# An attention and expert block on one core: expert slots moved into attention's last slot, the first lots cut anew, and the mask, state and read-out put in another order

## The chip, the cores and the metric

The kernel runs on one core of a Trainium2 chip, in one launch. The time is device microseconds of one execution, and the figure compared is the median of several. Five engines work side by side, each with its own queue in program order: PE (TensorE, matrix products), DVE (VectorE), ACT (ScalarE), POOL (GpSimd) and SP (SyncE, which here only issues DMAs). They wait for one another by semaphores.

## The reference

Four steps, each with a residual, on x of 4 x 1024 tokens by 128 (4096 tokens):

```
x = x + attn_a(layernorm(x))   # linear attention, H = 64: phi = elu + 1,
                               # S += k v^T, z += k, o = S q / max(z . q, 1e-6), then W_o
x = x + ffn(layernorm(x))      # 8 experts, top 1: gate * (relu(x W1[e] + b1[e]) W2[e] + b2[e])
x = x + attn_b(layernorm(x))   # 8 x 512: decayed running sum over tokens, mixed; sigmoid(r) * (v Wo)
x = x + ffn(layernorm(x))      # the same experts again
```

The expert of a token is the largest of its 8 router logits, which depend on the token's own row after attention; D_FF is 512. The reference computes all experts for all tokens and masks, the kernel only the chosen one.

## The kernel before

The 4096 tokens are 32 tiles of 128 rows (NT), in 8 groups of 4 tiles (NG, GT). **Attention** runs in slots k = 0 to 8 (`attn_slot(k)` on each engine, written out by hand). Slot k projects group k, forms scores and state of group k - 1, and reads out group k - 2 (`project_out`). On PE the order is: query and key projection (`project_qk`, L1661), read-out (L1763, L1767), scores and turns (L1693, L1681, L1704), transposes, value projection (L1670), state update and product within the chunk (L1714, L1723), product with the carried state (`read_inter`, L1743), and the count of chosen experts (`count`, L1644). On DVE it is: `add_attention` (dmax L979, then the new rows L996), the mask (L1118), then the choice of experts for batch k - 3 mixed with the statistics of group k - 2 and the addition of the state (L1131), then phi (qk, L1139), the placing of batch k - 3 (`placed`, L955 to L966), and the scan of z (L1146). ACT evacuates PSUM, takes exp and relu for phi, normalizes the next group (`norm`) and copies the read-out (`evac_o`, L702). POOL computes zq (L513) and the row scales (L505), and sends tiles of rows to their place in the sorted array in memory by indirect DMA (L532). SENDS_OF_ATTENTION says which tiles in which slot: 0 to 12 by slot 7, then 13, 14 to 19 in slot 8, 20 to 27 after it; the last four go among the expert slots.

**Experts** run in 39 slots (ST) of 128 sorted rows. A slot is: SP loads the rows (xs), DVE normalizes them (xsn, L1381), PE turns them (L1887), ACT copies the turned rows (xsT, L796), PE forms the first product (L1897), ACT, from slot 9 on with DVE, applies relu (hT, L801), PE forms the second product (L1911), DVE adds it to the row (L1411) and POOL scatters the result (L555). ACT also copies each slot's weights ahead (w1s, L719). Slots belong to lots (STAGES): a lot may be loaded when all rows of its batches are sent and its table (`table_step`: which expert and which tile each slot has) is done. In the first layer the lots have 9, 12 and 18 slots and end with batches 3, 6 and 7, so the first lot needs tiles 0 to 15. The first table is made by DVE in slot 8 (L1276 to L1316). PE does dummy products (`keep_clock`, L1780) in slot 8 and ahead of the first expert turn. After the first layer the rows come back from memory, the mixing runs in slots of its own, and a second set of 39 expert slots follows, with lots of 5, 8, 8 and 18.

## Time and profile before

| | |
|---|---|
| median of 3 runs | 287.8 us (287.49 to 288.69) |
| the profiled execution | 288.31 us, its span 286.6 us |
| PE busy | 270.5 us, 94% of the span |
| DVE busy | 227.2 us, 79% |
| POOL busy | 219.0 us, 76% |
| ACT busy | 183.8 us, 64% |
| mean granted clock of PE | 0.988 |
| attention slots | from 12.65 to about 70 us |
| first layer's experts | to about 151 us |
| mixing, then the second layer's experts | to the end |

The span is that of the trace; 1.7 us of the execution lie around it. Starts are counted from the span's start. The shares are means over stages in which different engines wait.

### The profile page before, as it was taken

The numbers are of one execution on the slowest core, as the hardware profiler recorded it, in microseconds if no ns is written. First come the engines' busy times: TensorE is split into PE (matmuls) and PEld (weight loads), VectorE is DVE, ScalarE is ACT, GpSimd is POOL, SyncE is SP. The second block draws the span as 40 slices with busy tenths as digits, with TensorE's granted clock in tenths as the row PEclk, the third lists the DMA queues.
The fourth block names the chain that finished last, engine by engine and source line by source line (L and its number), as shares of the span: only waits on it lengthen the run. The fifth ranks groups of instructions, "written<-read, shape, count | busy, mean of one in ns | idle before, by whom it ended". The sixth has DMA issues, their size and how long they took to land.

```text
span 286.6 us, 8102 instructions
## 1 busy us (share of the span) xinstructions
PE 270.5 (94%) x2343; PEld 239.6 (84%) x2343; DVE 227.2 (79%) x1030; ACT 183.8 (64%) x564; POOL 219.0 (76%) x304
## 2 busy tenths in 40 slices
PE   7989999987899999999999799999899999999994
PEld 7766666654598999999994488898699999999994
DVE  4797999997786987788771589999947988777873
ACT  2686666531599788888870276563289976676661
POOL 3956288777868898886553888888778888888875
PEclk9999999998999999999999999999899999999999
DMA  5799950011413655331103800101324244332210
GB/s 133 212 260 321 172 88 31 28 41 53 120 39 86 131 109 114 100 80 47 39 18 75 225 1 0 49 29 40 90 64 115 76 119 101 108 94 71 66 42 4
DMA packets 32652, 25.73 MB, mean 90 GB/s; under 512 B 6129, under 2 KB 28914, under 8 KB 32609
## 3 DMA queue, kind: packets, MB, share of 16 engines
q1 hardware_dynamic: 27456, 16.54, 25.5%
q0 software_dynamic: 4576, 8.57, 9.0%
q8 instruction: 20, 0.33, 0.5%
q14 instruction: 24, 0.19, 0.2%
q10 hardware_dynamic: 576, 0.10, 0.2%
HBM read 14.60 MB, written 11.57 MB: 91 GB/s over the span
## 4 chain that ended last, share of the span: by engine, by line
PE 63%; DVE 18%; DMA 5%; SPq 4%; issue 3%; POOL 3%; ACT 2%; DVEq 0%; ACTq 0%; POOLq 0%
PE pair L1911 21%; PE pair L1897 15%; PE bank L1897 7%; PE bank L1887 3%; SPq L374 3%; PE pair L1831 2%; DVE rows L996 2%; PE bank L1780 2%; DVE stats L1011 2%; PE pair L1763 2%; PE pair L1824 2%; PE pair L1661 2%; DMA rows<-x_mid 2%; DVE am L1118 1%; DVE sc L1220 1%
## 5 line engine op out<-in xcount | busy, mean ns | idle before, releaser
L1911 PE MATMUL pair<-w2s,hT 128*128 x624 | 82.7, 276 | 0.1
L532 POOL DMA_INDIRECT sorted<-rows,place x64 | 66.5, 1039 | 18.2 <-issue 14.9
L1911 PEld LDWEIGHTS pair<-w2s,hT 128*128 128x128 f32 x624 | 75.7, 192 | 0.4 <-issue 0.2
L1897 PE MATMUL pair<-xsT,w1s 128*128 128x128 f32 x406 | 57.7, 278 | 0.9 <-ACT xsT L796 0.9
L1897 PEld LDWEIGHTS pair<-xsT,w1s 128*128 128x128 f32 x406 | 51.5, 194 | 1.9 <-DVE tm L1229 1.0
L719 ACT COPY w1s<-w1all 128x516 f32 x78 | 49.7, 638 | 0.6 <-issue 0.4
L555 POOL DMA_INDIRECT x_mid<-ys,xs x39 | 38.5, 986 | 13.9 <-DVE ys L1421 9.4
L555 POOL DMA_INDIRECT out<-ys,xs x39 | 38.6, 989 | 9.1 <-issue 7.2
L796 ACT COPY xsT<-bank 128x128 f32<-128x128 f32 x78 | 20.8, 267 | 37.2 <-PE bank L1887 36.3
L1411 DVE SCALAR_TENSOR_TENSOR ys<-pair,xs 128x128 f32<-128x128 f32 x78 | 27.0, 347 | 21.3 <-PE pair L1911 20.9
L801 ACT ACTIVATE hT<-pair,w1s 128x128 f32<-128x128 f32 x117 | 34.8, 375 | 1.1 <-PE pair L1897 1.1
L801 ACT ACTIVATE hT<-bank,w1s 128x128 f32<-128x128 f32 x109 | 32.6, 377 | 0.0
L1897 PE MATMUL bank<-xsT,w1s 128*128 128x128 f32 x218 | 31.1, 278 | 0.4 <-ACT xsT L796 0.4
L1392 DVE SCALAR_TENSOR_TENSOR xs<-b2b,xs 128x128 f32<-128x128 f32 x78 | 27.3, 351 | 4.8 <-issue 2.7
L1381 DVE TENSOR_SCALAR xsn<-xs 128x128 f32<-128x128 f32 x78 | 28.0, 363 | 2.9 <-DMA xs<-sorted 2.9
L1897 PEld LDWEIGHTS bank<-xsT,w1s 128*128 128x128 f32 x218 | 28.0, 196 | 0.6 <-ACT xsT L796 0.6
L1401 DVE TENSOR_SCALAR hT<-pair,w1s 128x128 f32<-128x128 f32 x86 | 27.6, 346 | 0.7
L505 POOL TENSOR_TENSOR rows<-veps,neg_half 128x4 f32<-128x4 f32 x16 | 17.2, 1072 | 8.8 <-ACT veps L675 7.7
L563 POOL MEMSET idle_row<- 1x320 f32 x60 | 21.9, 364 | 0.0
L1887 PE MATMUL bank<-ident,xsn 128*128 128x128 f32 x78 | 21.5, 275 | 0.3 <-DVE xsn L1381 0.3
L1831 PE MATMUL pair<-wp,sc 128*128 128x256 f32 x64 | 16.3, 379 | 0.0
L1824 PE MATMUL pair<-wx,xnT 128*128 128x256 f32 x64 | 15.7, 388 | 0.6 <-DVE xnT L1201 0.6
(184 smaller groups left out, 499.3 us busy)
## 6 DMA issues: line engine op xcount, KB each, us to landing
xs<-sorted SPq DMA_DIRECT2D x78, 66.0 KB, 2.3
rows<-x_mid SPq DMA_DIRECT2D x8, 260.0 KB, 5.1
w1all<-in_L_ffn_W_b SPq DMA_DIRECT2D x8, 258.0 KB, 6.0
rows<-in_L_attn_a_x SPq DMA_DIRECT2D x16, 128.0 KB, 2.7
w2s<-in_L_ffn_W SPq DMA_DIRECT2D x8, 256.0 KB, 5.3
sorted<-pad SPq DMA_DIRECT2D x30, 66.0 KB
sorted<-rows,place POOLq DMA_INDIRECT x64, 2.6
x_mid<-ys,xs POOLq DMA_INDIRECT x39, 2.6
```

The source lines that it names most:

```text
L532: pool.indirect_dma_start(sorted_rows[l], bass.IndirectOffsetOnAxis(ap=place[:, t:t + 1], axis=0), rows[:, t, :], None).then_inc(s_sent[l] ...
L555: pool.indirect_dma_start(x_new[l], bass.IndirectOffsetOnAxis(ap=xs[b][:, IDC:IDC + 1].bitcast(I32), axis=0), ys[b][:, 0:(XM, D)[l]], None ...
L719: nc.scalar.copy(w1s[i % NW][:], w1all[:, bass.ds(e, 1), :].rearrange("p o f -> p (o f)")).then_inc(s_w1, 1)
L801: last = nc.scalar.activation(hT[i % NB][:, c], bank[2 + i % 2][:, c * P:(c + 1) * P], ACT.Relu, bias=w1s[i % NW][:, DF + c:DF + c + 1])
L1381: nc.vector.tensor_scalar(xsn[i % NB][:], xs[b][:, 0:D], xs[b][:, MEAN:MEAN + 1], xs[b][:, RSTD:RSTD + 1], ALU.subtract, ALU.mult).then_in ...
L1392: nc.vector.scalar_tensor_tensor(out=xs[b][:, 0:D], in0=b2b[:, bass.ds(e, 1), :].rearrange("p o d -> p (o d)"), scalar=xs[b][:, GATE:GATE ...
L1401: last = nc.vector.tensor_scalar(hT[i % NB][:, c], bank[4 + i % 2][:, f:f + P], w1s[i % NW][:, DF + c:DF + c + 1], 0.0, ALU.add, ALU.max)
L1411: nc.vector.scalar_tensor_tensor(out=ys[b][:, 0:D], in0=bank[6 + i % 2][:, 0:P], scalar=xs[b][:, GATE:GATE + 1], in1=xs[b][:, 0:D], op0=AL ...
L1831: last = nc.tensor.matmul(mix_to(g, j), sc[g % 2][:, j * P:(j + 1) * P], wp[:].rearrange("p w d -> p (w d)"), start=False, stop=(j % 2 == ...
L1887: nc.tensor.transpose(bank[0][:, 0:P], xsn[i % NB][:], ident[:]).then_inc(s_xsT, 1)
L1897: mm = nc.tensor.matmul(bank[2 + 2 * half + i % 2][:, c * P:(c + 1) * P], w1s[i % NW][:, f:f + P], xsT[i % NB][:], start=True, stop=True)
L1911: mm = nc.tensor.matmul(bank[6 + i % 2][:, 0:P], hT[i % NB][:, c], w2s[:, bass.ds(e, 1), c, :].rearrange("p o d -> p (o d)"), start=(c == ...
```

## The change

First layer only, with the line numbers of each program in the fences:

- **Lots.** The first layer gets the second's lots: 5, 8, 8 and 18 slots, that end with batches 2, 4, 6 and 7. The first needs tiles 0 to 11 only. SENDS_OF_ATTENTION is as before. Four tables are made in place of three.
- **Tables.** The first table's steps are dealt into slots 6 and 7 of attention (five and four steps), the second's into slot 8.
- **Slot 8.** DVE normalizes the rows of expert slots 0 and 1 right behind the mask. PE turns the first of them ahead of `read_inter`, and does the first product and the second turn ahead of the last `project_out`. ACT does the copies of both and the first relu in slot 8, ahead of the exp of batch 5 and `row_veps` of batch 6. The dummy products go (five in all).
- **All attention slots.** `project_qk(k + 1)` stands at the end of slot k, ahead of the count. The counts go to bank 2 and wait for `evac_v`; the value projection waits for the placing that read them, and `project_out` no longer does. On DVE the state is added ahead of the maximum of the logits, the mask is one instruction in place of two, and z's scan stands ahead of `placed`. On ACT `evac_o` stands ahead of `norm`.
- **Placing.** `placed` of batch 5 moves behind the last `add_attention`; its count behind the last `project_out`.
- **Start.** SP issues the six loads of the mixing weights behind x of group 3, ahead of x of groups 4 to 7. On DVE the moments of group 4 move into slot 0, those of group 6 into slot 1.

```diff
-STAGES = [[(3, 9), (6, 12), (7, 18)], [(2, 5), (4, 8), (6, 8), (7, 18)]]
+STAGES = [[(2, 5), (4, 8), (6, 8), (7, 18)], [(2, 5), (4, 8), (6, 8), (7, 18)]]
-        attn_counts = bank[7][:, 2 * YC:2 * YC + (GT + 1) * E]
+        attn_counts = bank[2][:, HW + P:HW + P + (GT + 1) * E]
...
                 for g in range(2, NG):
                     load_x(l, g)
+                    if l == 0 and g == 3:
+                        for dst, src in ((rwo, rw_o), (rwr, rw_r), (rwv, rw_v)):
+                            sp.dma_start(dst[:], src).then_inc(s_wmix, 16)
+                        for i, v in enumerate((time_decay, mix_v, mix_r)):
+                            sp.dma_start(vec[:, i:i + 1], v.rearrange("(h o) -> h o", o=1)).then_inc(s_wmix, 16)
...
+                if k == NG:
+                    copy_w1(0, 0)
                 if 0 <= k - 1 < NG:
                     evac_kv(k - 1)
+                if k == NG:
+                    evac_rows(0, 0)
+                    copy_w1(0, 1)
+                    evac_o(LASTG)
+                    relu(0, 0)
+                    evac_rows(0, 1)
+                    lexp(0, AS, LASTG - 2)
+                    row_veps(AS, LASTG - 1)
+                    return
...
                 row_stats(AS, g, 1)
                 bias_logits(0, AS, b)
                 row_stats(AS, g, 2)
+                add_state(g + 1)
                 max_logit(0, b)
...
-                if g + 1 < LASTG:
-                    add_state(g + 1)
...
                 if k == NG:
-                    table_sums(0, 0)
-                    table_experts(0, 0)
-                    add_state(k - 1)
-                    table_places(0, 0)
+                    normed_rows(0, 0)
+                    normed_rows(0, 1)
+                    measure_choose_and_list()
+                    return
...
                 phi(k)
+                scan_z(k)
                 if k - 3 >= 0:
                     placed(0, AS, k - 3)
-                scan_z(k)
                 if k == 0:
+                    first_moments(4)
+                    mix_weights(0)
                     first_moments(5)
+                if k == 1:
                     first_moments(6)
-                    mix_weights(0)
-                if k == 1:
                     first_moments(7)
...
                 if 0 <= k - 1:
                     updates_and_intra(k - 1)
+                if k == NG:
+                    turn_rows(0, 0)
                 if 0 <= k - 1:
                     read_inter(k - 1)
+                if k == NG:
+                    after(pe, AS["posb"], 2 * (LASTG - 3) + 1)
+                    first_product(0, 0)
+                    turn_rows(0, 1)
+                    return
+                if k + 1 < NG:
+                    project_qk(k + 1)
                 if 3 <= k < NG:
-                    pe.wait_ge(AS["xnew"], k - 1)
+                    pe.wait_ge(AS["v"], k + 1)
                     count(AS, k - 3, attn_counts)
-                if k == NG:
-                    count(AS, k - 3, bank[1])
...
                 if l == 0:
                     project_out(LASTG)
-                    keep_clock(3)
+                    count(AS, LASTG - 2, bank[1])
+                    pe.wait_ge(s_w2, 16 * (1 + E))
```

`measure_choose_and_list` is the choice of batch 5 and the statistics of group 6, with the end of the first table, the state, and all nine steps of the second table among them, in the order of the second layer's `choose_measure_and_list`.

On PE, in attention's last slot and behind it, before: vT is turned, then dummies on w2s, the state's update, the masked scores with kt, the state's product, the count; and after the read-out of the last group (wox) come more dummies, and only then the experts' turn (xsn) and first product (w1s).

```order
L1704 MATMUL bank<-ident,vT 128x128 x3
L1780 MATMUL bank<-w2s,ident 128x512 x2
L1714 MATMUL pair<-kt,vt 64x64 x2
L1723 MATMUL pair<-am,kt 64x128 x4
L1743 MATMUL pair<-qk,state 64x128 x4
L1644 MATMUL pair<-oh,before 128x32
```

```order
L1763 MATMUL pair<-wox,ob 128x137 x2
L1767 MATMUL pair<-ones_col,zq 128x1 x2
L1763 MATMUL pair<-wox,ob 128x137 x2
L1767 MATMUL pair<-ones_col,zq 128x1 x2
L1780 MATMUL bank<-w2s,ident 128x512 x3
L1887 MATMUL bank<-ident,xsn 128x128
L1897 MATMUL pair<-xsT,w1s 128x128 x4
L1887 MATMUL bank<-ident,xsn 128x128
L1897 MATMUL bank<-xsT,w1s 128x128 x4
L1887 MATMUL bank<-ident,xsn 128x128
```

And in the changed program:

```order
L1762 MATMUL bank<-ident,vT 128x128 x3
L1772 MATMUL pair<-kt,vt 64x64 x2
L1781 MATMUL pair<-am,kt 64x128 x4
L1943 MATMUL bank<-ident,xsn 128x128
L1801 MATMUL pair<-qk,state 64x128 x4
L1953 MATMUL pair<-xsT,w1s 128x128 x4
L1943 MATMUL bank<-ident,xsn 128x128
L1819 MATMUL pair<-wox,ob 128x137 x2
L1823 MATMUL pair<-ones_col,zq 128x1 x2
L1819 MATMUL pair<-wox,ob 128x137 x2
L1823 MATMUL pair<-ones_col,zq 128x1 x2
L1700 MATMUL pair<-oh,before 128x32
```

The first expert turn stands ahead of the state's product, the first product and second turn ahead of the last read-out, and the dummies are gone.

On ACT, in the same slot, before: the last kt and vt, the exp of batch 5 (le), the read-out (ob), veps of batch 6, then the first weights (w1s) and the first turned rows (xsT).

```order
L695 COPY kt<-pair 128x256
L696 COPY vt<-bank 128x384
L668 ACTIVATE le<-ld 128x32
L702 COPY ob<-pair 128x256
L675 ACTIVATE veps<-rows 128x4
L348 TENSOR_LOAD etab
L719 ISA
L719 COPY w1s<-w1all 128x516
L796 COPY xsT<-bank 128x128
L348 TENSOR_LOAD etab
```

And in the changed program:

```order
L696 COPY kt<-pair 128x256
L697 COPY vt<-bank 128x384
L803 COPY xsT<-bank 128x128
L348 TENSOR_LOAD etab
L720 ISA
L720 COPY w1s<-w1all 128x516
L703 COPY ob<-pair 128x256
L808 ACTIVATE hT<-pair,w1s 128x128 x4
L803 COPY xsT<-bank 128x128
L669 ACTIVATE le<-ld 128x32
L676 ACTIVATE veps<-rows 128x4
```

veps of batch 6, which POOL's row scale waits for, now stands behind the first relu (hT) and the second turned rows.

On DVE, around the start of slot 0 (phi gives qk, zT is the scan), before, with moments as stats and mv:

```order
L859 BN_STATS stats<-rows 128x6 x4
L864 BN_AGGR mv<-stats 128x2 x4
L1261 TENSOR_SCALAR whole<-capt 1x8 x2
L1139 SCALAR_TENSOR_TENSOR qk<-ex,rl 128x512
L1146 SCALAR_TENSOR_TENSOR zT<-ones_col,qk 128x256
L859 BN_STATS stats<-rows 128x6 x4
L864 BN_AGGR mv<-stats 128x2 x4
L859 BN_STATS stats<-rows 128x6 x4
L864 BN_AGGR mv<-stats 128x2 x4
L1361 COPY rwoT<-pair 128x128
L1362 TENSOR_SCALAR mix_c<-vec 128x2
```

And in the changed program:

```order
L1313 TENSOR_SCALAR whole<-capt 1x8 x2
L1194 SCALAR_TENSOR_TENSOR qk<-ex,rl 128x512
L1201 SCALAR_TENSOR_TENSOR zT<-ones_col,qk 128x256
L865 BN_STATS stats<-rows 128x6 x4
L870 BN_AGGR mv<-stats 128x2 x4
L1413 COPY rwoT<-pair 128x128
L1414 TENSOR_SCALAR mix_c<-vec 128x2
L865 BN_STATS stats<-rows 128x6 x4
L870 BN_AGGR mv<-stats 128x2 x4
L1173 TENSOR_TENSOR am<-pair,causal 128x512
L1422 TENSOR_SCALAR wx<-pair,vec 128x128
```

One set of moments has moved from ahead of qk to behind the scan, and the mask (am) is one instruction.

## Rows read from the trace of the kernel before

**Rows 1.** The page, part 1: busy us, share of the span, instructions.

```profile
PE 270.5 (94%) x2343; PEld 239.6 (84%) x2343; DVE 227.2 (79%) x1030; ACT 183.8 (64%) x564; POOL 219.0 (76%) x304
```

**Rows 2.** Timeline, attention slot 6: start us, duration us, engine, line, operation.

```profile
49.09 0.16 DVE L979 TENSOR_SCALAR dmax<-pair 128x4 f32<-128x4 f32 x1 [0.43 <-PE pair L1767]
...
52.95 0.65 PE L1743 MATMUL pair<-qk,state 64*64 64x128 f32 x8 [0.35 <-DVE state L1131]
...
55.94 0.16 DVE L979 TENSOR_SCALAR dmax<-pair 128x4 f32<-128x4 f32 x1 [0.47 <-PE pair L1767]
```

**Rows 3.** Timeline, attention's last slot and the first expert slots, PE and DVE.

```profile
61.24 0.50 PE L1763 MATMUL pair<-wox,ob 64*128 64x137 f32 x4 [0.56 <-DVE posb L955]
...
62.35 0.16 DVE L979 TENSOR_SCALAR dmax<-pair 128x4 f32<-128x4 f32 x1
...
63.90 0.74 DVE L1118 TENSOR_TENSOR am<-pair,causal 128x256 f32<-128x256 f32 x2
...
70.36 0.16 DVE L979 TENSOR_SCALAR dmax<-pair 128x4 f32<-128x4 f32 x1 [0.86 <-PE pair L1767]
...
71.92 0.59 DVE L1381 TENSOR_SCALAR xsn<-xs 128x128 f32<-128x128 f32 x2
...
72.53 0.35 DVE L1392 SCALAR_TENSOR_TENSOR xs<-b2b,xs 128x128 f32<-128x128 f32 x1
...
74.69 0.19 DVE L931 TENSOR_TENSOR oh<-rev,top 128x32 bf16<-128x32 f32 x1
...
74.80 1.13 PE L1897 MATMUL pair<-xsT,w1s 128*128 128x128 f32 x8 [0.45 <-ACT xsT L796]
...
77.63 1.14 PE L1911 MATMUL pair<-w2s,hT 128*128 x8
```

**Rows 4.** Timeline, the first attention slots, DVE and PE.

```profile
10.49 0.87 DVE L859 BATCH_NORM_STATS2 stats<-rows 128x6 f32<-128x128 f32 x4
...
12.65 0.69 DVE L1139 SCALAR_TENSOR_TENSOR qk<-ex,rl 128x512 f32<-128x512 f32 x1 [0.41 <-ACT rl L682]
...
16.02 0.33 PE L1875 MATMUL pair<-ident,rwo 128*128 128x128 f32 x1 [0.89 <-DMA vec<-in_L_attn_b_time_mix_r]
...
19.38 0.99 DVE L1139 SCALAR_TENSOR_TENSOR qk<-ex,rl 128x512 f32<-128x512 f32 x1
...
22.24 0.13 DVE L979 TENSOR_SCALAR dmax<-pair 128x4 f32<-128x4 f32 x1
```

**Rows 5.** Timeline, DVE in the second layer's slot with a table.

```profile
200.06 0.16 DVE L1321 TENSOR_SCALAR cover<-cumt 1x8 f32<-1x8 f32 x1
...
201.17 0.16 DVE L909 TENSOR_REDUCE mx<-lg 128x4 f32<-128x32 f32 x1
```

**Rows 6.** Timeline, ACT and POOL in the passage to the experts.

```profile
68.52 0.21 ACT L675 ACTIVATE veps<-rows 128x4 f32<-128x4 f32 x1 [0.27 <-DVE rows L1017]
...
72.66 1.06 POOL L532 DMA_INDIRECT sorted<-rows,place  x1 [0.30 <-issue]
...
76.24 1.15 ACT L801 ACTIVATE hT<-pair,w1s 128x128 f32<-128x128 f32 x4
...
77.25 0.65 ACT L719 COPY w1s<-w1all 128x516 f32 x1
```

**Rows 7.** Timeline, the opening of the second lot: PE, POOL, DVE.

```profile
79.50 0.27 PE L1887 MATMUL bank<-ident,xsn 128*128 128x128 f32 x1
...
85.38 0.96 POOL L532 DMA_INDIRECT sorted<-rows,place  x1 [0.30 <-issue]
...
90.93 0.35 DVE L1381 TENSOR_SCALAR xsn<-xs 128x128 f32<-128x128 f32 x1 [2.29 <-DMA xs<-sorted]
...
91.33 0.33 PE L1887 MATMUL bank<-ident,xsn 128*128 128x128 f32 x1 [0.30 <-DVE xsn L1381]
```

**Rows 8.** Windows: busy us of each engine, granted clock, DMA share, GB/s.

```profile
66.00:69.00 3.00, 1.09 (x17) 0.79 (x19) 2.65 (x19) 0.70 (x3) 1.67 (x3) 1.00 0.14 47
69.00:73.00 4.00, 4.00 (x20) 2.54 (x19) 3.05 (x15) 0.62 (x1) 3.19 (x4) 0.57 0.37 95
```

More of the change, by code:

```diff
@@ L1095, in measure_choose_and_add_state @@
                 scale_logits(0, AS, b)
+                if b == LASTG - 4:
+                    table_step(0, 0, "tiles")
+                if b == LASTG - 3:
+                    table_step(0, 0, "experts")
+                    table_step(0, 0, "jumps")
                 row_stats(AS, g, 1)
@@ L1109, in measure_choose_and_add_state, with measure_choose_and_list @@
                 row_moments(AS, g, 2)
+                if b == LASTG - 4:
+                    table_step(0, 0, "past")
+                    table_step(0, 0, "jump")
                 one_hot(0, AS, b)
                 row_moments(AS, g, 3)
+            def measure_choose_and_list():
+                b, g = LASTG - 2, LASTG - 1
+                sum_logits(b)
+                dve.wait_ge(AS["xnew"], g + 1)
+                table_step(0, 0, "cover")
+                row_stats(AS, g, 0)
+                scale_logits(0, AS, b)
+                table_step(0, 0, "taken")
+                row_stats(AS, g, 1)
+                table_step(0, 1, "tiles")
+                bias_logits(0, AS, b)
+                table_step(0, 1, "round")
+                row_stats(AS, g, 2)
+                add_state(g + 1)
+                max_logit(0, b)
+                table_step(0, 0, "behind")
+                row_stats(AS, g, 3)
+                table_step(0, 1, "sum")
+                lead_logits(0, AS, b)
+                dve.wait_ge(AS["st2"], 2 * g + 1)
+                row_moments(AS, g, 0)
+                table_step(0, 1, "past")
+                table_step(0, 1, "jump")
+                rank_leaders(0, AS, b)
+                row_moments(AS, g, 1)
+                table_step(0, 1, "experts")
+                top_rank(0, b)
+                table_step(0, 1, "jumps")
+                row_moments(AS, g, 2)
+                one_hot(0, AS, b)
+                table_step(0, 1, "skips")
+                row_moments(AS, g, 3)
+                table_step(0, 1, "places")
             def mask_scores(g):
@@ L1572, in _ @@
             norm_half()
-            for g in range(2, 5):
+            for g in range(2, 4):
                 first_moments(g)
```

177 lines of the change are left out of this document (85 added, 92 removed).

## The prediction, made before the changed kernel ran

> **What bounds the kernel now.** I read the busy shares of the page first: TensorE (PE) is busy 94% of the span, VectorE (DVE) 79%, GpSimd (POOL) 76%, ScalarE (ACT) 64% [rows 1]. This is an average over stages, so I read the timeline by stage. In the attention part one slot, counted from dmax to dmax, takes 6.85 us (slot 6: 49.09 to 55.94), and two engines wait little in it: PE stands 0.35 us before the read of the state (L1743), waiting for DVE's state, and DVE stands 0.47 us before dmax (L979), waiting for PE's read-out [rows 2]. So PE's own work is about 6.85 - 0.35 = 6.5 us a slot and DVE's about 6.85 - 0.47 = 6.4 us: whoever gets a wait removed hands the bound to the other 0.1 us later. Then comes the passage to the experts: from dmax of attention's last slot (62.35) to the first second product (77.63) it is 15.28 us [rows 3]. From there PE runs without a gap at 1.9 us a slot, but for one stall at the opening of the second lot (turn at 91.33) [rows 7]. So the layer is a chain of DVE and PE to 62.35, a passage of waits, and then PE alone; what changes the end is when the second products begin, how fast PE's clock is there, and whether each lot's rows are in time. The second layer isn't edited, and I let it move as a block.
>
> **Part 1, the start of attention.** The six mix loads go ahead of x of group 4, so PE no longer waits for them (0.89 us before L1875 [rows 4]). This gives little: ACT is the next in line, since the router weights now stand behind the projection of slot 1, and I find the transposes of slot 1 at the same time within 0.2 us. The cost is on DVE. The moments of group 4 lie now in a hole: they start at 10.49 and DVE waits again for 0.41 us at 12.65 for ACT's rl [rows 4]. They move behind that point, where DVE goes without long waits up to dmax of slot 2 at 22.24. One set of moments is 0.87 of stats and 0.38 of aggregates, 1.25 us [rows 4]. Against it: qk of slot 1 takes 0.99 us while POOL's zq runs beside it, and 0.69 us at 12.65 [rows 4]; zq(0) now comes later, because the moments of group 5, for which POOL's scales of groups 4 and 5 wait ahead of it, now stand behind those of group 4 and the mix weights; so this 0.3 us is saved. Sum **+1.0 us** at dmax of slot 2; bounds 0 (if a wait that I don't see absorbs it) and +1.4.
>
> **Part 2, slots 3 to 5.** DVE adds the state before the maximum and the last stats, 0.4 us earlier, so PE's 0.35 us go; the mask in one instruction of 512 columns in place of two saves DVE one fixed part, 0.06 us. The slot becomes PE's 6.5 us. **-0.36 us** each in three slots, -1.1 together; I take -1.15 since one of the three had a wait of this kind and one for the one-hot. Bounds 0 and -1.4 (DVE's floor). The read-out copied ahead of the norm delays ACT's exp and relu by up to the norm; they end just before PE's turn of k needs them, so I cost it at nothing, at worst 0.2 a slot.
>
> **Part 3, slots 6 and 7.** Here the first table is dealt in. In the second layer a stretch with four such steps, nine instructions from cover to the maximum, takes 1.11 us [rows 5], 0.12 each in the mean; the steps are its smallest, so I take 0.08 to 0.1 each. Five steps in slot 6 make DVE's slot 6.4 - 0.06 + 0.4 = 6.7 (before 6.85), four in slot 7 make it about 6.75 where before it was 62.35 - 55.94 = 6.41 [rows 2, 3]: -0.1 and **+0.33**. DVE is the bound here, so all of it counts. The scan of z also stands before the placing now, so that POOL's zq runs beside DVE's pick. The row of slot 1 says that such a neighbour can cost 0.3 us (0.99 against 0.69 [rows 4]); I add **+0.3** for both slots, bounds 0 and 0.8.
>
> The Trainium skill, "SBUF — State Buffer", section "Who interferes with whom", says that a DVE instruction with two SBUF inputs and a GpSimd instruction that reads SBUF block one another for their length. By that rule alone pick would wait for most of zq in each slot and the sum would be 0.5 us worse; the trace agrees for qk, and shows no pick beside a zq.
>
> Parts 1 to 3: +1.0 - 1.15 - 0.1 + 0.33 + 0.3 = **+0.4 us**: dmax of slot 8 at 62.75.
>
> **Part 4, the passage.** Counted from dmax of slot 8. The mask ends at 64.64 - 62.35 - 0.06 = 2.23 [rows 3]. Two normed rows, 0.35 each less overlap: 2.85; I see no wait for their load, since lot one needs only tiles 0 to 11 (sent by slot 7) and a table that is done in slot 7. Sum of logits, then cover to the maximum in 1.11 [rows 5]: 4.05; state 0.2: 4.25. PE reads it in 0.65 (52.95 [rows 2]): 4.95; first product 1.1 (1.13 [rows 3]): 6.05; turn 0.1; read-out 1.11 (61.24 to 62.35 [rows 3]): 7.25. The read-out (project_out(7)) now stands behind expert work, and DVE, through with its list at about 6.3, waits 0.9 us for it. From dmax to the new rows' end 71.92 - 70.36 = 1.56, with the pipeline's tail 1.65: 8.9. Placing of batch 5, five small instructions, 0.65: 9.55. From hidden(0) to the one-hot of batch 6 74.88 - 72.53 = 2.35, less a pause of 0.1 [rows 3]: 11.8; with 0.2 us for the register load ahead of hidden: 12.0. Count and semaphores 0.2: the first second product at **12.2** in place of 15.28, **-3.1 us**. What went are the table and the placing ahead of DVE's last add_attention, and the first turn and product behind it, with the dummies; what is late next is the one-hot of batch 6, as the count ahead of the second product waits for it. Bounds -3.5 (DVE's dependent chain faster) and -2.0 (a semaphore of 0.1 us for each of ten hops more).
>
> ACT: row_veps(6) stands behind relu(0,0), which waits for the first product. It is at 6.05 + 1.15 (four relus [rows 6]) + 0.5 = 7.7 in place of 68.52 - 62.35 = 6.17. POOL's scale waits for it, and tiles 17 to 19 are queued behind: tile 19 is sent at 11.6 in place of 72.66 - 62.35 = 10.31 [rows 6]. Afterwards ACT stands for row_veps(7) until DVE's moments of group 7 (about 14.0), and in these slots ACT is as long as PE (1.15 of relu, 0.65 of copy [rows 6] and the evacuation): a slip of **+0.2 us**.
>
> **Part 5, the lots.** From sending a lot's last tile to the turn of its first slot it is 91.33 - 85.38 = 5.95 us [rows 7]. Second lot: 11.6 + 5.95 = 17.55, wanted by PE at 12.2 + 5.6 = 17.8, so just in time. Third lot: tile 27 goes as now at about 85.4 on POOL, which loses 1.3 us by the veps and no longer has to wait as long for the placing of batch 6; wanted four slots later than now, so it fits by 5 us. The stall of the second lot goes: turns stand at 79.50 and 91.33, six slots, 11.83 us, of which 6 x 1.9 = 11.4 are slots: **-0.45 us**. Last lot as now with 2 us less of slack; POOL's scatters catch up before the layer's end.
>
> **Part 6, PE's clock.** The granted clock was 1.00 from 66 to 69 us with PE busy 1.09 of 3 us, and 0.57 in the mean over 69 to 73: it stood at its lower level, 1.2 GHz, for about 3.4 us, then came back to 2.4 [rows 8]. Today that falls on the dummy products. Now they are gone, and PE has 1.7 us idle ahead of turn(2) and again 1.5 ahead of the count, between 8.6 and 12.0. I expect the same fall, and the lower level to last into the first two slots. A low stretch of 3.4 us costs 1.7 if all of it is work; about a quarter lies on the idle part: **+1.3 us**. Bounds 0 and 3.4 (two stretches). The Trainium skill, "TensorE: Matmul & The Clock Gate", section "HAM oscillation", says that PE left idle between bursts drops to half its clock and begins the next burst cold. The trace agrees with it [rows 8]. By that rule alone both idle pieces count, the term is its bound of 3.4, and the sum ends 2.1 us higher, at 288.1.
>
> **Sum**, against the profiled execution (288.31 us, span 286.6): +0.4 - 3.1 + 0.2 - 0.45 + 1.3 = -1.65, so 286.65. That execution lies 0.5 us above the median of the three runs, 287.8; against the median I get 286.1, and say **286.0**.
>
> **Rivals.** (a) The clock holds or is low only while PE idles: 1.3 less, 284.7. For it: the work in the passage is denser than between 66 and 68.5 us. Against it: two idle pieces one after the other. Chance 0.2. (b) The clock stays low for a second stretch, since the first finds PE half idle: 1.7 more, 287.7. Chance 0.15. (c) The gain of the attention slots doesn't come, or the mid-passage hops are dearer: parts 2 and 4 at their near bounds, +1.5, 287.5. Chance 0.1. (d) The change doesn't do what it says: PE waits at the second lot. The place is tile 19 behind row_veps(6); it decides from 0.25 us on (17.8 less 17.55), and from about 2 us on the stall costs its length and, with PE idle that long, another low stretch of 1.7: 286.0 + 2 + 1.7 = 289.7, slower than before. For it: POOL is back to back there, and every microsecond of relu goes into it. Against it: 5.95 is measured end to end. Chance 0.13. The forecast, 285.2 to 287.0, has 0.42.
>
> **Range.** 284.0 to 289.0: from (a) with part 1 at zero to the edge of (d). Under and over it I leave 0.2. A measurement tells 0.5%, 1.4 us, from no change: faster is below 286.4, most of the forecast and (a), 0.55; same is the rest of the forecast, (b) and (c), 0.31; slower is (d) and a little of (b), 0.14.
>
> **What would show it.** Part 1: dmax of slot 2 near 23.2. Part 2: no wait of PE before the state in slots 3 to 5, dmax 6.5 us apart. Part 3: 6.7 in slots 6 and 7; a pick of over 0.3 us would show the neighbour. Part 4: dmax of slot 8 at 62.8, the first second product 12.2 after it, DVE idle ahead of the last dmax. Part 5: no wait for xs at the sixth and fourteenth slot. Part 6: a granted clock of 0.5 between about 73 and 77 us. The prediction is wrong if the first second product comes before 73.5 or after 76.5, or if turn(5) waits.

## The result, and the profile after

The changed kernel takes **289.5 us** (median of 17 executions, 288.0 to 292.9) where the kernel before takes 287.8 beside it (17 executions, 285.3 to 290.2). The ratio is 1.0068, 95% interval 1.0038 to 1.0098: 0.7% slower, where 286.0 and a gain were forecast. Here and in the table below, the ratios leave out executions over 1.5% above the fastest of their kernel, and the medians take in all, so that a ratio isn't quite the quotient of two medians. The profiled execution took 289.96 us (span 288.2).

The page of the changed kernel, PE's rows of the overview by slices:

```profile
span 288.2 us, 8098 instructions
PE 269.7 (94%) x2333; PEld 240.4 (83%) x2333; DVE 227.9 (79%) x1035; ACT 183.6 (64%) x564; POOL 219.3 (76%) x305
...
PEclk9999999995579999999999999999999999999999
```

The busy shares are those of [rows 1]. What is new stands in the clock row: two and a half slices of 7.2 us with PE's clock well under full. The windows of PE in the passage (window, its length, PE busy and its instructions, granted clock, DMA share, GB/s):

```profile
60.00:64.00 4.00, 3.18 (x42) 1.00 0.21 53
64.00:68.00 4.00, 2.32 (x20) 0.71 0.34 91
68.00:72.00 4.00, 4.00 (x27) 0.50 0.10 34
72.00:76.00 4.00, 2.79 (x21) 0.50 0.05 17
76.00:80.00 4.00, 1.76 (x10) 0.50 0.18 53
80.00:84.00 4.00, 4.00 (x26) 0.66 0.55 137
```

In the kernel before the low stretch was 3.4 us long [rows 8]; here it is 17.1 (twice the sum of 1 minus the clock, over windows of 1 us). Its start, in the timelines of PE, DVE, ACT and POOL (start, duration, engine, line, operation, in brackets the idle time ahead and what ended it):

```profile
63.37 0.13 DVE L985 TENSOR_SCALAR dmax<-pair 128x4 f32<-128x4 f32 x1
63.54 0.49 PE L1762 MATMUL bank<-ident,vT 128*128 128x128 f32 x3
65.71 0.48 PE L1772 MATMUL pair<-kt,vt 128*64 128x64 f32 x4 [1.68 <-DVE am L1173]
68.50 2.07 PE L1953 MATMUL pair<-xsT,w1s 128*128 128x128 f32 x8
71.89 0.23 ACT L676 ACTIVATE veps<-rows 128x4 f32<-128x4 f32 x1
72.76 0.16 DVE L985 TENSOR_SCALAR dmax<-pair 128x4 f32<-128x4 f32 x1 [3.50 <-PE pair L1823]
75.59 0.35 DVE L1447 SCALAR_TENSOR_TENSOR xs<-b2b,xs 128x128 f32<-128x128 f32 x1 [0.55 <-issue]
76.05 0.98 POOL L533 DMA_INDIRECT sorted<-rows,place  x1 [0.30 <-issue]
76.26 0.48 PE L1943 MATMUL bank<-ident,xsn 128*128 128x128 f32 x1 [1.47 <-DVE xsn L1432]
77.87 0.19 DVE L937 TENSOR_TENSOR oh<-rev,top 128x32 bf16<-128x32 f32 x1
78.32 0.18 PE L1700 MATMUL pair<-oh,before 128*128 128x32 bf16 x1 [1.58 <-DVE oh L937]
78.99 2.07 PE L1976 MATMUL pair<-w2s,hT 128*128 x8 [0.39 <-issue]
```

PE waits 1.68 us for the mask, just where the two dummy products stood (63.40 in the kernel before), and from there on it runs at 1.2 GHz: a first product takes 2.07 us in place of 1.13 [rows 3]. From 65.71 to 74.78 PE worked without any idle time, and the clock did not come back. The first second product comes 15.62 us after dmax of slot 8, not 12.2, and only at 82.7 is the clock full again.

The last second products of the layer, kernel before first, then changed:

```profile
148.87 2.15 PE L1911 MATMUL pair<-w2s,hT 128*128 x16
151.41 2.15 PE L1976 MATMUL pair<-w2s,hT 128*128 x16
```

By stages the 1.6 us between the two spans are: dmax of slot 2 +0.67 (22.24 to 22.91), the slots to dmax of slot 8 +0.35, the passage +0.34, the second products of the first layer +1.18 (71.24 to 72.42), the way to the second layer's second products -1.84, these themselves +0.88, the rest 0.02. The last two aren't the change's. This execution of the kernel before had a low stretch of 3.4 us at 205 to 210 us; in the four traces of either program that have one between 201 and 210 the way takes 60.4 to 60.8 us and the second layer's second products 71.3, in the fourteen others 58.9 to 59.4 and 72.0 or more. So of its own the change loses 2.5 us in this trace, all in the first layer; the medians lie 1.8 us apart.

### The profile page after: what moved, and what is told of

It is laid out like the page before. It is cut to its first block, busy times and chain, and to the rows that moved or that the text cites. A ratio compares the mean times of both kernels' runs of the same rounds, so it can differ in the third digit from the quotient of the medians.

```text
span 288.2 us, 8098 instructions
## 1 busy us (share of the span) xinstructions
PE 269.7 (94%) x2333; PEld 240.4 (83%) x2333; DVE 227.9 (79%) x1035; ACT 183.6 (64%) x564; POOL 219.3 (76%) x305
## 4 chain that ended last, share of the span: by engine, by line
PE 67%; DVE 23%; issue 3%; POOL 3%; ACT 2%; DMA 2%; DVEq 0%; POOLq 0%; SPq 0%; ACTq 0%
PE pair L1976 24%; PE pair L1953 16%; PE bank L1953 8%; PE bank L1943 3%; DVE rows L1002 3%; PE pair L1831 3%; PE pair L1890 2%; PE pair L1883 2%; DVE stats L1017 2%; DVE zT L1201 2%; PE bank L1690 1%; DVE qk L1194 1%; DVE am L1173 1%; DVE sc L1272 1%; DVE rows L1023 1%
## 5 line engine op out<-in xcount | busy, mean ns | idle before, releaser
L1976 PE MATMUL pair<-w2s,hT 128*128 x624 | 83.9, 278 | 0.7 <-issue 0.6
L533 POOL DMA_INDIRECT sorted<-rows,place x64 | 66.4, 1037 | 17.1 <-issue 15.6
L1976 PEld LDWEIGHTS pair<-w2s,hT 128*128 128x128 f32 x624 | 76.6, 194 | 1.5 <-issue 1.2
L1953 PE MATMUL pair<-xsT,w1s 128*128 128x128 f32 x406 | 58.8, 282 | 0.4 <-ACT xsT L803 0.4
L1953 PEld LDWEIGHTS pair<-xsT,w1s 128*128 128x128 f32 x406 | 52.6, 197 | 1.3 <-DVE tm L1281 1.0
L803 ACT COPY xsT<-bank 128x128 f32<-128x128 f32 x78 | 20.8, 266 | 39.9 <-PE bank L1943 38.9
L506 POOL TENSOR_TENSOR rows<-veps,neg_half 128x4 f32<-128x4 f32 x16 | 16.8, 1048 | 12.4 <-ACT veps L676 12.2
```

The lines of the kernel that those rows point to most:

```text
L533: pool.indirect_dma_start(sorted_rows[l], bass.IndirectOffsetOnAxis(ap=place[:, t:t + 1], axis=0), rows[:, t, :], None).then_inc(s_sent[l] ...
L1953: mm = nc.tensor.matmul(bank[2 + 2 * half + i % 2][:, c * P:(c + 1) * P], w1s[i % NW][:, f:f + P], xsT[i % NB][:], start=True, stop=True)
L1976: mm = nc.tensor.matmul(bank[6 + i % 2][:, 0:P], hT[i % NB][:, c], w2s[:, bass.ds(e, 1), c, :].rearrange("p o d -> p (o d)"), start=(c == ...
```

## The experiments

All runs were compared with the kernel before on the same chip. In the table: the median of the executions, the ratio to the kernel before with its interval, and from the one trace of each the length of the low stretches (up to 284 us), dmax of slots 2 and 8, and the first second product. Each row has 12 executions, but for the first two (17), and after_again, all_held and the last three with 6. The runs were made in four groups, each on another chip: hold_once to zq_late, after_again to all_four, held_zq_late to all_held, and the last four; the kernel before had medians of 288.8, 289.1, 289.6 and 289.1 us beside them. Executions of one kernel lie up to 9 us apart (285.8 to 294.9), and one took 343. So the traces carry the reasons and the ratios the weight, and small differences between groups say little.

| kernel | us | ratio | low, us | dmax 2 | dmax 8 | second product |
|---|---|---|---|---|---|---|
| before, first trace | 287.8 | | 3.4 + 3.4 | 22.24 | 62.35 | 77.63 |
| changed, first trace | 289.5 | 1.0068 (1.0038-1.0098) | 17.1 | 22.91 | 63.37 | 78.99 |
| hold_once | 289.0 | 1.0038 (0.9989-1.0088) | 6.8 + 3.4 | 22.35 | 63.14 | 78.50 |
| hold_thrice | 289.0 | 1.0030 (0.9982-1.0078) | 3.4 | 22.80 | 63.25 | 76.24 |
| before_bare | 287.9 | 1.0022 (0.9986-1.0058) | 10.2 | 21.67 | 61.76 | 77.44 |
| zq_late | 288.4 | 1.0043 (0.9997-1.0090) | 3.4 | 22.55 | 61.98 | 75.73 |
| after_again | 290.1 | 1.0102 (1.0040-1.0165) | 10.2 + 3.4 | 22.37 | 63.13 | 78.57 |
| count_late | 288.6 | 1.0011 (0.9971-1.0050) | 3.4 + 13.7 | 22.81 | 64.65 | 78.29 |
| count_zq_sends | 288.6 | 0.9990 (0.9936-1.0043) | 6.8 + 6.8 | 22.30 | 61.74 | 75.76 |
| all_four | 285.4 | 0.9923 (0.9878-0.9968) | 3.4 + 10.2 | 22.95 | 63.77 | 76.14 |
| held_zq_late | 288.5 | 0.9978 (0.9937-1.0020) | 3.4 + 3.4 | 23.17 | 63.99 | 77.38 |
| start_old | 288.9 | 0.9982 (0.9944-1.0020) | 17.1 | 21.82 | 62.52 | 78.13 |
| before_zq_first | 292.1 | 1.0076 (1.0027-1.0124) | 3.4 | 22.23 | 64.49 | 79.82 |
| all_held | 285.6 | 0.9880 (0.9824-0.9937) | 3.4 | 23.05 | 63.71 | 73.87 |
| start_zq_old | 289.5 | 1.0035 (1.0001-1.0069) | 17.1 | 22.90 | 62.65 | 78.92 |
| start_zq_held | 285.5 | 0.9888 (0.9837-0.9940) | 3.4 | 21.74 | 61.37 | 74.74 |
| all_start_held | 284.5 | 0.9868 (0.9816-0.9919) | 3.4 | 21.81 | 61.19 | 71.00 |
| all_moments_held | 285.1 | 0.9873 (0.9828-0.9918) | 3.4 | 22.79 | 62.25 | 72.03 |

### The dummy products

My theory was that the clock is the loss; the rivals, DVE's slots in attention and the later idle pieces. Two dummy products back in slot 8 (hold_once), and one each ahead of the third turn and of the count as well (hold_thrice):

```diff
                 if k < NG:
                     project_v(k)
+                if k == NG:
+                    pe.wait_ge(s_w2, 16 * (1 + E))
+                    keep_clock(2)
                 if 0 <= k - 1:
                     updates_and_intra(k - 1)
```

> The changed kernel with two dummy products put back in slot 8, ahead of the state update, so that PE is busy behind the mask (64.0 to 65.7 us). Theory (the clock): the granted clock stays at 1.00 over 66 to 74 us, first product and read-out take 1.1 us each in place of 2.1 and 1.9, the first second product comes about 76 in place of 78.99, and the time is 286 to 287.5. Rival 1 (the loss is on DVE in the attention slots): the clock may hold, but the first second product moves by less than 0.5 us and the time stays at 289 to 290. Rival 2 (the idle pieces ahead of the third turn and of the count are enough by themselves): the clock falls later, near 72 to 76 us, and the time is about 288.5.

> As with two dummy products in slot 8, and one more each ahead of the third turn and of the count of batch 6. Theory (the clock): no low stretch at all up to the second products, the first of them at 75.8 to 76.5, 285.5 to 287. Rival 1 (DVE): 289 to 290 with the clock at 1.00. Rival 2 (later idle pieces matter by themselves): this one is faster by 1 to 2 us than the kernel with the two dummies of slot 8 alone; if the two are within 0.5 us of each other, rival 2 falls.

In the trace of hold_once the clock fell at 61.0, ahead of the dummies; the passage took 15.36 us. In that of hold_thrice it held up to 75.7, and the passage took 12.99. Both medians lie over the 286 to 287.5 expected, and neither ratio can be told from the changed kernel's.

The granted clock that every execution reports says more than one trace. Twice the span times what the clock lacks of 1 is the low time of that execution (with up to 2 us at the program's very end, which the table leaves out). In the 17 executions of the changed kernel it is 6.9 to 23.9 us, 13.8 in the median, and the time follows it: the three with 6.9 us took 288.0 to 288.2, the five with 17.4 or more took 290.0 to 292.9. A straight line through the 17 gives 0.26 us for each us of low clock, so 3.6 us for the 13.8, as an estimate. In hold_once the median is 10.4 us, in hold_thrice 9.2, in the kernel before beside them 6.9. So the dummies took only a quarter to a third of the low time away, and the traced execution of hold_thrice (286.81 us, where the median is 289.0) was the second fastest of its twelve.

One idle piece that the dummies don't reach stands a slot earlier. The changed kernel's PE waits 1.13 us for the mask of slot 7, where it was 0.30 in the kernel before:

```profile
58.98 0.55 PE L1772 MATMUL pair<-kt,vt 128*64 128x128 f32 x8 [1.13 <-DVE am L1173]
```

In hold_once and after_again, two of the six traces that have it, the clock fell at 61, behind this wait (1.15 and 1.13 us) and one of 0.65. With the scan of z late it is 0.57, and in none of those traces did the clock fall between 28 and 64 us. No run takes this piece out by itself.

In the kernel before, the other way round, I took all five dummies out:

> The kernel before without its dummy products of attention's last slot (two) and ahead of the first turn (three); all else as before. Theory (the clock): PE idles about 2 us behind the mask and again behind the read-out, the clock falls to 0.5 near 65 us and stays there into the first slots, and the kernel becomes 2 to 4 us slower, 290 to 292. Rival 1 (DVE's chain sets the passage and PE's clock hardly matters there): within 0.7 us of the kernel before, 287 to 288.5.

The clock fell, for 10.2 us, and no cost can be told: the interval goes from 0.9986 to 1.0058, the median of all executions is 287.9 beside 288.8, and the passage took 15.68 us against 15.28. The windows of before_bare:

```profile
64.00:68.00 4.00, 1.57 (x25) 0.83 0.15 51
68.00:72.00 4.00, 2.02 (x21) 0.50 0.32 75
72.00:76.00 4.00, 3.12 (x12) 0.50 0.54 130
76.00:80.00 4.00, 4.00 (x37) 0.89 0.27 72
```

There PE stands idle for 4.1 us of the stretch, 2.1 of them for DVE's rows behind the table, and the clock is full again as the second products begin. So a low clock by itself is no price; it counts where PE is what the others wait for. Whether it is one in the changed kernel was still open. The changed kernel again, on the second group's chip, showed that its first trace was no accident:

> The changed kernel itself, unchanged, once more, beside the kernel before and the three below on one chip. Theory (where PE idles behind the mask in slot 8 with nothing to bridge it, the clock falls there and stays low for long): the granted clock is at 0.50 for over 10 us between 64 and 84 us again, the fastest execution stays above 287, the median is 289 to 290.5. Rival (where the clock falls is chance, and the 17 us of the first trace were bad luck): a low stretch of 3.4 or 6.8 us, and executions down to 285.5 as of the kernel with zq late.

Low for 13.6 us around the passage, in two stretches, none of six executions under 289.2, 1.0% slower.

### The neighbour of the scan

```diff
                 phi(k)
-                scan_z(k)
                 if k - 3 >= 0:
                     placed(0, AS, k - 3)
+                scan_z(k)
```

> The changed kernel with the scan of z behind the placing again, as before; all else as changed. Theory (pick and POOL's zq get in each other's way): pick of slot 6 takes 0.2 in place of 0.80 us, dmax of slot 8 comes 0.4 to 0.7 us earlier, but the low clock stays, and the time is 288.6 to 289.2. Rival (the neighbour only moves to qk, or PE waits longer for zq): no difference, 289.2 to 290.

> The kernel before with this one part of the change: the scan of z ahead of the placing, so that POOL's zq runs beside DVE's pick. Theory (the neighbour costs the same wherever it stands): pick takes up to 0.8 us in some slots, the six slots from dmax to dmax take 40.8 to 41.4 us in place of 40.1, and the time is 0.2 to 0.4% above the kernel before. Rival (in the kernel before DVE has 0.47 us of wait ahead of dmax, which swallows it): 40.1 to 40.4 and no difference.

Slot 6 of the changed kernel, DVE and POOL, then the pick of zq_late:

```profile
55.61 0.80 DVE L965 TENSOR_TENSOR pick<-posb,oh 128x32 f32<-128x32 f32 x1
55.64 0.71 POOL L514 TENSOR_TENSOR zq<-zT,qk 128x256 f32<-128x256 f32 x1
```

```profile
54.22 0.25 DVE L965 TENSOR_TENSOR pick<-posb,oh 128x32 f32<-128x32 f32 x1
```

Pick takes 0.80 us beside zq and 0.25 without, as long as zq plus its own 0.1. From dmax of slot 2 to dmax of slot 8 it is 40.11 us in the kernel before, 40.46 and 40.76 in the changed kernel, and 39.43 in zq_late: the order costs 1.0 to 1.3 us in the traces. A good half is the pick of slot 6 (that slot 7.27 against 6.70), the only one that runs beside zq; in the other slots pick takes 0.19 to 0.28 us. Of the rest slot 4 has 0.48 (6.93 against 6.45), while slot 3 is 0.22 shorter, and I can't put it to one instruction. In the kernel before the same edit costs 2.15 us (42.26), where pick accounts for 0.56 (0.75 against 0.19 in slot 6): there PE's read-out waits for the placing, which now stands behind the scan, 0.27 to 0.31 us ahead of dmax of slots 4 to 7 and 1.32 ahead of that of slot 8:

```profile
48.99 0.50 PE L1763 MATMUL pair<-wox,ob 64*128 64x137 f32 x4 [0.31 <-DVE posb L955]
```

### The start

```diff
                 if k == 0:
-                    first_moments(4)
-                    mix_weights(0)
                     first_moments(5)
-                if k == 1:
                     first_moments(6)
+                    mix_weights(0)
+                if k == 1:
                     first_moments(7)
...
-            for g in range(2, 4):
+            for g in range(2, 5):
                 first_moments(g)
```

and the six mix loads behind x of group 7 again (start_old).

> The changed kernel with the start of attention as before: mix loads behind x of group 7, moments of group 4 in the hole ahead of the first projection, moments of groups 5 and 6 ahead of the mix weights. Theory (the moved moments cost what they last): dmax of slot 2 at 21.7 to 22.3 in place of 22.4 to 22.9, PE waits 0.9 us for the mix weights again without harm, all later marks 0.5 to 0.7 us earlier. Rival (the start is absorbed later, since PE or ACT is the bound there): dmax of slot 8 within 0.2 us of the changed kernel's 63.1 to 63.4.

Dmax of slot 2 comes at 21.82, and the ratio is 0.998 with the 17.1 us of low clock untouched: under the changed kernel's in both its comparisons. By the ratios more than DVE's 0.7 us goes here, but these comparisons are on different chips, and the medians are only 0.7 and 1.2 us under the changed kernel's two; how much more is not shown. The start in the changed kernel (POOL, then PE), and PE in all_held:

```profile
19.32 1.61 POOL L580 DMA_INDIRECT x_mid<-pad  x1 [0.18 <-issue]
20.95 0.74 POOL L514 TENSOR_TENSOR zq<-zT,qk 128x256 f32<-128x256 f32 x1
21.79 0.51 PE L1819 MATMUL pair<-wox,ob 64*128 64x137 f32 x4 [1.07 <-issue]
```

```profile
21.75 0.50 PE L1825 MATMUL pair<-wox,ob 64*128 64x137 f32 x4 [1.80 <-issue]
...
22.00:26.00 4.00, 4.00 (x33) 0.57 1.11 341
```

POOL's zq of group 0 stands behind the scales of groups 4 and 5, which now wait for the later moments; it ends at 21.69, in the kernel before (19.06, 0.74 us) at 19.80, and PE's first read-out waits for it. In six of the ten traces with the changed order PE idles 1.07 to 1.11 us there, and in four 1.80; in those four (count_late, all_four, held_zq_late, all_held) the clock falls, for 3.4 us, and slot 2 takes 7.6 to 7.8 us in place of 6.4. With the old order of the moments PE doesn't idle there.

The price of the old order is PE's wait for the mix loads at 15 to 17 us: 0.89 us [rows 4], 1.37 in start_old, 2.93 in start_zq_old, whose dmax of slot 2 slid to 22.90. Moments in the old order with the loads early (all_moments_held, below) don't help: DVE then waits 2.07 us for x of group 4, and dmax of slot 2 is at 22.79.

```profile
12.42 0.87 DVE L865 BATCH_NORM_STATS2 stats<-rows 128x6 f32<-128x128 f32 x4 [2.07 <-DMA rows<-in_L_attn_a_x]
```

### What the clock costs in the changed passage

> The changed kernel with both suspected faults taken out: the dummy products in slot 8 and one each ahead of the third turn and the count, and the scan of z behind the placing. Theory (these two are the whole loss): dmax of slot 8 at 61.9 to 62.2, low stretches of 3.4 to 6.8 us in all, the first second product 13.0 to 13.8 us after dmax of slot 8, and the time 0.2 to 0.8% under the kernel before on the same chip. Rival (something of the change that neither touches, the start or the start of the second lot, costs too): at or above the kernel before, ratio 1.000 or more.

Two faults out, 0.2% under the kernel before, but not told from it: the low stretch at the start hit this trace, and the low time of its twelve executions is still 9.4 us in the median. To get the clock's own price I took start and neighbour out of both, and ran them side by side without and with the dummies:

> The changed kernel with the start of attention as before and the scan of z behind the placing; no dummy products. Theory A (the loss is made in attention, at the start and by the neighbour, and the passage gains whatever the clock does): dmax of slot 2 at 21.7 to 22.0, of slot 8 at 61.1 to 61.5, the first second product at 75 to 76.5, and 0.6 to 1.0% under the kernel before. Theory B (the loss is the low clock in the passage): the clock is low for over 10 us in the passage and the time is within 0.3% of the kernel before.

> As the run before, with the dummy products in slot 8 and ahead of the third turn and the count. Theory A: no further gain, within 0.3% of the run before. Theory B: 0.7% or more faster than the run before, 0.8 to 1.2% under the kernel before, with a low stretch of at most 6.8 us.

This settles what the clock costs in this program. 1.0035 without, 0.9888 with, on one chip: **1.5% or 4 us for four dummy products** in otherwise the same program. Every execution bears it out: their low time is 10.9 to 20.8 us without and 0 to 8.6 us with them. For the changed kernel itself, with its own start and scan, the same dummies gave 0.4 to 0.7% by the ratios (hold_thrice, 1.0030 against 1.0068 and 1.0102), on other chips and not told apart, and left 9.2 us of low time; there the 4 us stay an estimate from the traces and from the straight line through the 17 executions. The windows of start_zq_old, then of start_zq_held:

```profile
64.00:68.00 4.00, 1.65 (x19) 0.80 0.43 111
68.00:72.00 4.00, 4.00 (x27) 0.50 0.09 30
72.00:76.00 4.00, 2.71 (x21) 0.50 0.05 17
76.00:80.00 4.00, 1.83 (x11) 0.50 0.18 57
80.00:84.00 4.00, 4.00 (x23) 0.56 0.50 124
```

```profile
64.00:68.00 4.00, 3.00 (x38) 1.00 0.43 103
68.00:72.00 4.00, 2.89 (x29) 1.00 0.02 6
72.00:76.00 4.00, 2.74 (x14) 0.86 0.15 51
76.00:80.00 4.00, 4.00 (x28) 0.72 0.51 118
80.00:84.00 4.00, 4.00 (x38) 1.00 0.51 121
```

From dmax of slot 8 to the last second products it is 89.10 us without and 85.40 with them. Theory A, that the loss was all in attention, falls: with start and neighbour undone and the clock low the kernel is still no faster than before. But they matter for the clock: only with them undone too, or with the four edits below, did the dummies bring the low time under 5 us in the median (3.7 in start_zq_held and in all_held).

### A version that beats both

Behind the last dmax the first second product waits for the count of batch 6, of which it needs nothing. count_late puts the count behind the third first product:

```diff
                         first(i + 1)
+                    if i == 1 and l == 0:
+                        count(S, LASTB - 1, bank[1])
                     if i + 2 < ST:
                         turn(i + 2)
...
-                    if i == 0 and l == 0:
-                        count(S, LASTB - 1, bank[1])
                     second(i)
```

count_zq_sends has zq late too and sends tiles 17 to 19 ahead of POOL's row scale; all_four also puts DVE's third normed rows and first biased rows into its idle piece ahead of the last dmax, and the first add of y ahead of moments and placing; all_held adds the two dummies of slot 8; all_start_held and all_moments_held undo all of the start, or only its moments.

> The changed kernel with the count of batch 6 behind the first second product and the third first product, in place of ahead of both. Theory (at full clock the one-hot of batch 6 is what the first second product waits for, 5.3 us behind the last dmax, and it needs none of it): the first second product comes 3.5 to 4 us after the last dmax in place of 6.2, the second one about 2 us earlier than now, PE has one idle piece less, and the time is 1.3 to 2.2 us under the changed kernel's. Rival 1 (the second lot's rows then bind): the turn of slot 5 waits over 1 us, and less than 0.7 us is left of it. Rival 2 (the clock): with the low stretch as long as now the second products are slow, and the gain is under 1 us.

> The count late as in the run before, the scan of z behind the placing, and tiles 17 to 19 sent ahead of POOL's row scale of batch 6, so that they no longer wait for ACT's veps. Theory: dmax of slot 8 at 62.0, tile 19 sent 70 to 71 us in place of 76.05, no wait at the turn of slot 5, the first second product at 73.3 to 73.8 with the clock at 1.00, and 282.5 to 285. Rival (sending first only delays the row scale, and the third lot waits): the turn of slot 13 waits over 0.5 us, or the time is not under that of the kernel with the count late alone.

> As the run before, and on DVE the normed rows and the biased rows of the first slots (two instructions and their register load of 0.55 us) in the idle piece ahead of the last dmax, and the first add of y ahead of the moments of group 7 and the placing of batch 6. Theory: PE runs from the last dmax on with no idle piece over 0.5 us, the first second product comes 2 to 3 us after the last dmax (71.5 to 72.5), the clock holds up to there, and the time is 281.5 to 284, faster than the kernel before. Rival (DVE becomes the bound of the first slots): PE waits 1 us or more for ys or normed rows between 74 and 82 us, and the time is that of the run before within 0.7 us.

> The kernel with all four edits (count late, scan of z late, tiles 17 to 19 first, DVE's early rows) and the two dummy products in slot 8. Theory: PE has no idle piece over 0.7 us from 62 to 80 us, the clock stays low for 6.8 us at most, the first second product comes at 72.5 to 74, and the time is 282.5 to 285, 1.2 to 2% under the kernel before. Rival (the clock is set by the pieces ahead of slot 8, not by this one): low for 10 us again and no faster than the run with the four edits alone (0.992 of before).

> The kernel with the four edits of the passage and the dummy products, and the start as before. Theory (POOL's first scatter and scales ahead of zq make PE idle 1.1 to 1.8 us at 20 to 22 us in the changed kernel, and the clock sometimes falls there): no idle piece of PE over 0.6 us at 20 to 22 us, no low stretch there, all marks 0.7 us earlier from dmax of slot 2 on, the first second product at 72 to 73, and 1.4 to 1.9% under the kernel before. Rival (the start is swallowed by a later wait): 1.2%, as with the four edits and the dummies alone (0.988).

> As the run before, but only the order of DVE's moments is as before; the mix loads stay ahead of x of group 4. Theory (the cost of the start is the moved moments, not the loads): as the run before within 0.2%, and PE's wait of 0.9 to 1.4 us for the mix loads at 15 us is not there. Rival (the moments of group 4 in the hole wait for their x behind the mix loads): DVE waits over 0.5 us for x of group 4 near 10.5 us and dmax of slot 2 is later than 22.2.

The count late brings the first second product to 4.2 us behind the last dmax, from 6.2, near the 3.5 to 4 expected; but the clock was low for 13.7 us in that trace. The median is 1.4 us under that of after_again on the same chip, which has six executions only. count_zq_sends missed its 282.5 to 285: its trace has two stretches of 6.8 us of low clock, and a wait of 2.40 us ahead of the third turn. With all four edits PE waits 1.57 and 1.35 us up to 68.5 and then works without an idle piece up to 80; the median is 3.2 us under that of count_zq_sends on the same chip, from DVE's early rows and first add alone, and 0.8% under the kernel before, though its trace has the clock low for 10.2 us. all_start_held is the fastest, **284.5 us, ratio 0.9868 (0.9816 to 0.9919)**, its clock full over the whole passage:

```profile
71.00 1.15 PE L1983 MATMUL pair<-w2s,hT 128*128 x8 [0.84 <-DVE rows L1001]
...
68.00:72.00 4.00, 3.00 (x33) 1.00 0.18 55
72.00:76.00 4.00, 2.79 (x24) 1.00 0.34 83
76.00:80.00 4.00, 2.95 (x25) 1.00 0.56 131
```

Against all_moments_held, which differs in the place of the mix loads alone, the ratio says no more than 0.1%, within the interval; the trace says 1.0 us (71.00 against 72.03). Against all_held (0.9880, another chip) the old start can't be told in the ratio either.

## Why the prediction was wrong, by its own steps

- **Part 1, +1.0.** Measured +0.67 at dmax of slot 2 in the first trace (22.30 to 23.17 over the ten with this start), so the size was right. What failed is how I used zq(0): I saw that it comes later and counted only the 0.3 us that this saves qk (it did: 0.68 us). I didn't ask who waits for zq: PE's read-out, 1.07 to 1.80 us, with the low stretch behind it in four of ten traces.
- **Part 2, -1.15.** Measured -0.34 over slots 3 to 5, and -0.69 with zq late. DVE had no idle left to give: in the first trace of the changed kernel it has no wait over 0.2 us ahead of dmax in slots 3 to 7, and the slots are as long as its work. I took the 0.47 us ahead of dmax [rows 2] as its slack in each slot.
- **Part 3, +0.53** with the neighbour's 0.3. Measured +0.74 over slots 6 and 7. The steps came 0.17 us under their size (13.32 us with zq late, where 13.26 + 0.23 were forecast). The scan's new place cost 0.68 in these two slots, inside my bound of 0.8, and 1.0 to 1.3 over all six, where I had priced two. Where pick ran beside zq the rule of the Trainium skill, "SBUF — State Buffer", section "Who interferes with whom", was the better guide for its length: it has pick wait out zq, and pick did, 0.80 us beside 0.71. But the two met in slot 6 only, not in each slot as I had it by that rule.
- **Part 4, -3.1.** Up to the last dmax I forecast 7.25 us; at full clock it is 7.06 (hold_thrice) to 7.45. Behind it I forecast 4.95 and it is 5.93 to 6.30: DVE stands 0.55 us ahead of the biased rows, where their register load is, in place of 0.2, and behind the count PE stands another 0.4 us ahead of the second product, where its register load is, which in the kernel before lay under other work. The passage at full clock is 13.0 to 13.8 us, a gain of 1.5 to 2.3 where my near bound was 2.0: only hold_thrice's 12.99 lies inside. ACT's order had the effect described: in zq_late veps starts 7.55 us and tile 19 goes 11.77 us behind dmax of slot 8, forecast 7.7 and 11.6 (in the changed kernel, at the low clock, 8.52 and 12.68). What the slip itself costs no run shows.
- **Part 5, -0.45.** Right: no turn waits in the changed kernel's second or third lot, nor in start_zq_held, where PE is 4.3 us earlier.
- **Part 6, +1.3.** The step that failed. I forecast one fall of 3.4 us between 73 and 77. It fell at 65.6, behind the wait for the mask that the removed dummies had covered, a place that I didn't list among the idle pieces (in after_again at 61, a slot earlier), and was low for 17.1 and 13.6 us in the two traces. It costs 1.9 to 2.3 us ahead of the last dmax (9.39 against 7.45 in zq_late and 7.06 in hold_thrice) and some 1.8 in the first second products (3.7 us at half the rate), 4 in all; the pair of start_zq_old and start_zq_held gives as much in the medians, and the line through the 17 executions 3.6. The section "HAM oscillation" of "TensorE: Matmul & The Clock Gate" in the Trainium skill, by which an idle PE starts its next burst at half its clock and I had a term of 3.4 and 288.1, was nearer.
- **The rivals.** (a) fell: in every changed order without dummies the clock was low while PE worked. In the trace of zq_late it did what Part 6 forecast, one stretch of 3.4 us from 75.2, and that execution took 285.84 us; but the median of its twelve is 288.4, with 9.7 us of low time. (b) had the mechanism and about half the size. (c) came about: parts 2 and 4 fell short by 0.8 and 1.1 us. It was also wrongly added up: the two near bounds lie 2.25 us from the forecast, not 1.5. (d) fell: the second lot is in time, and the loss of 289.7 that it named came from elsewhere.

So the sum was -1.65 and the change's own part of the trace +2.5. The 4.2 us between them: start -0.3, slots +1.0, passage at full clock +1.1, clock +2.8, lots and ACT's slip -0.4. The last is what is left over, and the split between passage and clock is that of hold_thrice's trace.

## What to carry to other kernels

A dummy product is to be priced by the program that is to run, not by the one it stands in: here five of them were worth nothing that could be told before the change, and four of them 1.5% after it once the start and the scan were as before, since the low clock then lay on work on which the end depends. List every idle piece of PE that the new order opens, those of 1 to 2 us behind another engine's step first, and fill them with real work (the four edits without dummies gave 0.9923, with two of them 0.9880). Read the granted clock of all executions before taking one trace for the kernel. When a step is found to come later, ask who waits for it before counting what it frees.

## What the runs showed of the hardware

- The granted clock, once at 0.50, stayed there through 9.07 us of PE's work without an idle piece (65.71 to 74.78 us, changed kernel), and in the whole for up to 17.1 us. I had expected dense work to bring it back at once.
- Where the clock falls changes from execution to execution: at 61, 64 to 67, or 75 us in traces whose attention part is the same within a microsecond or two, and executions of one kernel spread over 1 to 3%. One trace tells where a low stretch lies; how long the clock is low in the others, the granted clock of each execution tells (0.959 to 0.988 in the 17 of the changed kernel).
- A vector instruction of 32 columns, 0.19 us alone, took 0.80 us beside a GpSimd product of 0.71 (pick and zq, slot 6 of the changed kernel).
- The second layer's second products, which no run edits, took 71.3 to 74.4 us; the longest has a turn that waits 2.38 us for its rows (before_bare, at 217 us). What delays these rows in some executions stays open.
